# Second layer's experts: the bias of the down product by one f32r matmul of ones against its high and low parts

## The reference, cut to what matters

```python
def _L1_ffn_ref(x, Wr, W1, b1, W2, b2):
    B, T, D, F_FF, E, K = (8, 512, 256, 1024, 8, 2)
    pooled = x.mean(axis=1)
    logits = pooled @ Wr
    top_scores, top_idx = jax.lax.top_k(logits, K)
    weights = jax.nn.softmax(top_scores, axis=-1)
    W1s, b1s = (W1[top_idx], b1[top_idx])
    W2s, b2s = (W2[top_idx], b2[top_idx])
    h = jnp.einsum('btd,bkdf->bktf', x, W1s) + b1s[:, :, None, :]
    h = jax.nn.gelu(h, approximate=False)
    y = jnp.einsum('bktf,bkfd->bktd', h, W2s) + b2s[:, :, None, :]
    return jnp.einsum('bk,bktd->btd', weights, y)
```

## Time and profile before

| | before |
|---|---|
| runs (us) | 3388.6, 3382.0, 3391.19; median 3388.6 |
| the profiled execution: span (us) | 3419.0 |
| TensorE busy over the span | 3115.7 us, 91% |
| mean granted TensorE clock | 0.957 of full speed |
| this stage (first bias matmul to last) | 1389.14 to 1583.18 us |

### The profile page before, as it was taken

The page is one execution under the profiler, slowest core; times in us unless marked ns, Lnnn a source line. Parts: engine busy times, 40 slices in busy tenths (PEclk is TensorE's granted clock), DMA queues, the critical chain, the costliest instruction groups (busy, mean ns, idle before and its releaser), DMA issues. The chain is left out here.

```text
span 3419.0 us, 59989 instructions
## 1 busy us (share of the span) xinstructions
PE 3115.7 (91%) x23982; PEld 2628.8 (77%) x23993; DVE 1875.7 (55%) x3913; ACT 1705.1 (50%) x3695; POOL 1520.5 (44%) x1146
## 2 busy tenths in 40 slices
PE   6997999999698898998997989799997999889995
PEld 5776888888575565897665868678886888789995
DVE  4764222223566465776554754467775666565554
ACT  4763332332276554554654653356665666535553
POOL 0222344434212675674234651233334454539984
PEclk9998999999799999999998999899999999999998
DMA  1002000100000010442001010110001000036652
GB/s 65 3 11 79 19 19 19 38 1 1 23 3 23 1 50 1 149 168 75 3 3 43 8 50 1 39 50 1 1 1 38 6 6 1 26 115 217 223 181 74
DMA packets 49794, 156.96 MB, mean 46 GB/s; under 512 B 9322, under 2 KB 29438, under 8 KB 37104
## 3 DMA queue, kind: packets, MB, share of 16 engines
q1 hardware_dynamic: 45776, 142.90, 12.2%
q0 software_dynamic: 3744, 10.23, 1.0%
HBM read 142.06 MB, written 10.26 MB: 45 GB/s over the span
## 5 line engine op out<-in xcount | busy, mean ns | idle before, releaser
L1303 POOL TENSOR_TENSOR prob<-prob,inv 128x512 f32<-128x512 f32 x320 | 331.6, 1042 | 401.3 <-DVE inv L1355 391.8
L1193 ACT ACTIVATE prob<-banks,nmax 128x256 f32<-128x256 f32 x640 | 297.3, 474 | 155.1 <-DVE nmax L1349 155.0
L2682 POOL TENSOR_TENSOR hL<-product,hH 128x512 fp32r<-128x512 f32 x128 | 165.9, 1296 | 321.5 <-ACT hH L2629 321.5
L2288 DVE TENSOR_REDUCE nmax<-banks 128x4 f32<-128x1024 f32 (+1 forms) x192 | 217.5, 1133 | 153.7 <-PE banks L1870 85.9
L2727 DVE TENSOR_TENSOR product<-banks,silu 128x512 f32<-128x512 f32 x128 | 88.6, 692 | 388.6 <-PE banks L2553 333.4
L2621 ACT ACTIVATE silu<-banks 128x512 f32<-128x512 f32 x128 | 76.5, 598 | 367.6 <-PE banks L2553 367.6
L1349 DVE TENSOR_REDUCE nmax<-banks 128x2 f32<-128x512 f32 x320 | 215.4, 685 | 20.6 <-PE banks L1172 16.2
L2553 PE MATMUL banks<-xH,upH 128*128 128x512 f32 x512 | 202.1, 395 | 5.8 <-POOL upL L2669 5.8
L2553 PE MATMUL banks<-xL,upH 128*128 128x512 f32 x512 | 201.5, 394 | 0.0
L2553 PE MATMUL banks<-xH,upL 128*128 128x512 f32 x512 | 199.9, 390 | 0.0
L3364 ACT ACTIVATE banks<-banks 128x512 f32<-128x512 f32 x124 | 71.9, 584 | 213.9 <-PE banks L3308 186.8
(11 more groups left out here) (617 smaller groups left out, 11026.6 us busy)
## 6 DMA issues: line engine op xcount, KB each, us to landing
W<-in_L_ffn_experts SPq DMA_DIRECT2D x80, 1024.0 KB, 5.4
W<-in_L_ffn_experts SPq DMA_DIRECT2D x8, 1536.0 KB, 7.9
slots_y<-W SPq DMA_DIRECT2D x23, 256.0 KB, 6.1
W<-strips SPq DMA_DIRECT2D x4, 768.0 KB, 7.5
W<-in_L_ffn_experts SPq DMA_DIRECT2D x9, 256.0 KB, 4.9
X<-in_x SPq DMA_DIRECT2D x1, 2048.0 KB, 8.3
cs<-in_ctxT SPq DMA_DIRECT2D x16, 128.0 KB, 2.3
W<-in_L_ffn_experts SPq DMA_DIRECT2D x1, 2048.0 KB, 7.6
```

The costliest lines, as they stand in the source:

```text
L1193: ins = nc.scalar.activation(m_.prob[p % 2][:, e * 512 + j * S:e * 512 + (j + 1) * S], bank(key)[:, j * S:(j + 1) * S], ACT.Exp, bias=m_.n ...
L1303: nc.gpsimd.tensor_tensor(pr, pr, m_.inv[:, slot(p, e):slot(p, e) + 2].unsqueeze(2).to_broadcast([P, 2, S]), ALU.mult)\
L2288: nc.vector.tensor_reduce(m_.nmax[b % 2][:, 2 * parts * i_:2 * parts * (i_ + 1)].rearrange("p (e q) -> p e q", e=2), scores.rearrange("p e ...
L2682: nc.gpsimd.tensor_tensor(m_.hL[:, at], m_.product[s % 2][:, :], m_.hH[:, at].bitcast(F32), ALU.subtract).then_inc(g.h_low.sem, 1)
```

## The change

The row of ones becomes a full f32r tile `ones_rows` of 128x128. For each k a tile `b2[k]` of 128x256 f32r is cleared once, and for each unit its row 0 gets the high part of b2 (ScalarE) and its row 32 the low part: ScalarE first writes the high part there too, and GpSimd then subtracts it from b2. One f32r matmul of the ones against that tile, taken twice, adds up the rows. b2 is loaded into rows 0 and 32 of `bcast`, so there is one more small load for each unit. The two copies of ScalarE stand between hidden 0 and hidden 1. GpSimd's subtraction stands behind the low part of the down weights, with a wait for it and a wait for the copies ahead, and a wait for itself behind. TensorE waits for GpSimd's result in place of its wait for the small loads; its wait for the low part of the down weights stays.

```diff
--- before.py
+++ after.py
@@ -211,6 +211,7 @@
         self.split_high, self.values_low = sig("narrow_weights_high"), sig("value_weights_low")
         self.xt_high, self.packed = sig("inputs_high"), sig("identity_packed")
         self.res_biased = sig("residual_biased")
+        self.b2_cleared, self.b2_high, self.b2_low = sig("down_bias_cleared"), sig("down_bias_high"), sig("down_bias_low")
 
     def expert_memory(self, scope, name):
 
@@ -2818,6 +2819,8 @@
         self.upH, self.upL = [sb("upH0", 2048), sb("upH1", 2048)], [sb("upL0", 2048), sb("upL1", 2048)]
         self.downH, self.downL = [sb("downH0", 2048), sb("downH1", 2048)], [sb("downL0", 2048), sb("downL1", 2048)]
         self.hH, self.hL = sb("hH", 2048), sb("hL", 2048)
+        self.ones = sb("ones_rows", P)
+        self.b2 = [sb("b2_0", D), sb("b2_1", D)]
 
 
 def experts_by_batch(nc, g, name, n, scope):
@@ -2873,7 +2876,8 @@
                     filled(sp, ("y", j - 2))
                 sp.dma_start(g.cols[:, k * 8:k * 8 + 8], g.dram[f"{name}.b1"][ds(e, 1), :, :].rearrange("a p c -> (a p) c"))\
                     .then_inc(g.half_loaded[k].sem, 16)
-                sp.dma_start(g.bcast[0:1, k * D:(k + 1) * D], g.dram[f"{name}.b2"][ds(e, 1), :]).then_inc(g.half_loaded[k].sem, 16)
+                for row in (0, 32):
+                    sp.dma_start(g.bcast[row:row + 1, k * D:(k + 1) * D], g.dram[f"{name}.b2"][ds(e, 1), :]).then_inc(g.half_loaded[k].sem, 16)
                 if j == 1:
                     prefetch(nc, g, sp, n + 1)
 
@@ -2918,9 +2922,9 @@
                     transpose_x(b + 1)
                 split(pe, g.down_low, j)
                 to = claim(("y", j))
-                loaded(pe, g.half_loaded, j, 32)
-                nc.tensor.matmul(to[:, :].rearrange("p (t d) -> p t d", t=2), g.ones[:, :],
-                                 g.bcast[0:1, k * D:(k + 1) * D].unsqueeze(1).to_broadcast([1, 2, D]), start=True, stop=False)
+                split(pe, g.b2_low, j)
+                nc.tensor.matmul(to[:, :].rearrange("p (t d) -> p t d", t=2), m_.ones[:, :],
+                                 m_.b2[k][:, :].unsqueeze(1).to_broadcast([P, 2, D]), start=True, stop=False)
                 for f in range(8):
                     if f % 2 == 0:
 
@@ -2968,9 +2972,13 @@
             down_high(0)
             act.wait_ge(g.chosen_ready.sem, g.chosen_ready.base + 1)
             nc.scalar.activation(ex, ex, ACT.Exp).then_inc(g.act_step.sem, 1)
+            act.wait_ge(g.b2_cleared.sem, g.b2_cleared.base + 1)
             for j in range(NU):
-                loaded(act, g.half_loaded, j, 32)
+                loaded(act, g.half_loaded, j, 48)
                 hidden(j, 0)
+                for row in (0, 32):
+                    ins = nc.scalar.activation(m_.b2[j % 2][row:row + 1, :], g.bcast[row:row + 1, (j % 2) * D:(j % 2 + 1) * D], ACT.Copy)
+                ins.then_inc(g.b2_high.sem, 1)
                 hidden(j, 1)
                 if j + 1 < NU:
                     up_high(j + 1)
@@ -2987,6 +2995,9 @@
                 pool.wait_ge(g.var_ready.sem, g.var_ready.base + b + 1)
                 nc.gpsimd.tensor_tensor(g.rstd[:, 2 * b:2 * b + 2], g.vare[:, 2 * b:2 * b + 2], g.mhalf[:, 0:2], ALU.pow).then_inc(g.rstd_ready.sem, 1)
 
+            nc.gpsimd.memset(m_.ones[:, :].bitcast(F32), 1.0)
+            nc.gpsimd.memset(m_.b2[0][:, :].bitcast(F32), 0.0)
+            nc.gpsimd.memset(m_.b2[1][:, :].bitcast(F32), 0.0).then_inc(g.b2_cleared.sem, 1)
             for j in range(NU):
                 if j:
                     split(pool, g.up_high, j + PIECES - 1)
@@ -2996,6 +3007,11 @@
                 nc.gpsimd.tensor_tensor(m_.downL[j % 2][:, :], raw[j % 2][:, 2048:4096], m_.downH[j % 2][:, :].bitcast(F32), ALU.subtract)\
                     .then_inc(g.down_low.sem, 1)
                 b, k = divmod(j, 2)
+                split(pool, g.down_low, j)
+                split(pool, g.b2_high, j)
+                nc.gpsimd.tensor_tensor(m_.b2[k][32:33, :], g.bcast[32:33, k * D:(k + 1) * D], m_.b2[k][32:33, :].bitcast(F32), ALU.subtract)\
+                    .then_inc(g.b2_low.sem, 1)
+                split(pool, g.b2_low, j)
                 if k == 0 and b:
                     power(b - 1)
             power(B - 1)
@@ -3074,7 +3090,10 @@
     for k in range(2):
         g.up_loaded[k].base += 16 * B
         g.down_loaded[k].base += 16 * B
-        g.half_loaded[k].base += 32 * B
+        g.half_loaded[k].base += 48 * B
+    g.b2_cleared.base += 1
+    for sig in (g.b2_high, g.b2_low):
+        sig.base += NU
     g.var_ready.base += B
     g.rstd_ready.base += B
```

## The result

The changed kernel took 3368.13 us (median of 5 runs, 3364.47 to 3372.84), beside 3385.41 us (5 runs) of the kernel before: ratio 0.9944, 95% interval 0.993 to 0.9957. Two later comparisons, each on one chip, gave 0.9946 (0.9933 to 0.9958) and 0.9950 (0.9934 to 0.9965). By these ratios it is faster by 17 to 19 us (the medians lie 17.3, 20.2 and 17.8 us apart); forecast were 15.3 us, a time of 3373.3 us, and a range of 3366 to 3384.

A forecast was written before the change was run, and what follows sets the result against it. TensorE was taken to bound the experts' stage; a cheaper bias saves 7.2 us in seven units and 8.1 in eight, none in unit 0: 3388.6 - 15.3 = 3373.3 us, range 3366 to 3384.

The forecast's parts named there:

- What bounds it: Experts' stage: TensorE, busy for all 194.04 us between the first and last bias matmul, sets the time.
- The new matmul: TensorE's bias in each unit: one f32r matmul at 0.23 us replaces 1.26 or 1.24 us, saving 1.03 or 1.01.
- Rival 2: TensorE's bias: new matmul overlaps with nothing, 0.4 us per unit, 6.4 us less gain, 3379.7; chance 0.13 together with Rival 1.
- The copies: ScalarE between hidden 0 and hidden 1: two one-row copies, 0.72 us per unit, bounds 0 and 0.81, mostly hidden.
- The subtraction: GpSimd, one row of 256 per unit: 0.63 us, hidden with 1.9 us of slack before TensorE's bias in unit 3.
- VectorE's slack in unit 3: VectorE's low parts ahead of TensorE's down product: 0.4 us left for piece 0, 0.6 for piece 1, nothing late.
- Rival 1: Units with k = 1: VectorE or ScalarE becomes late, at worst 6 us lost, 3380; chance 0.13 together with Rival 2.
- Unit 0: First unit, where VectorE's first low part is late: no gain, taken as 0; a blocked small operation would lose 0.3 us.
- Sum: Whole stage: 7 x 1.03 plus 8 x 1.01 us, unit 0 nothing, 15.3 us saved.
- the 5 us allowed for the spread: Lower end of the time range: 5 us for run spread, beside the full saving and a lower matmul price, giving 3366.

The follow-up runs named there:

- e1: The changed kernel with TensorE's bias put back to the plain fp32 matmul of one row of ones; ratio to the kernel before 0.9995.
- e5: The changed kernel with its f32r bias matmul taking row 0 alone, low part left out of the result; ratio to the kernel before 0.997.
- e11: The changed kernel with its bias matmul reading the same 128-row tiles as plain fp32 instead of f32r; ratio to the kernel before 0.9977.
- e2: The changed kernel without its bias matmul, loads, copies, subtraction and waits kept; ratio to the kernel before 0.9947.
- e3: The changed kernel with each of ScalarE's two copies of b2 made twice, the second into an unread tile; ratio to the kernel before 0.9957.
- e6: The changed kernel with the high part of b2 alone: no second ScalarE copy, no GpSimd subtraction; ratio to the kernel before 0.9947.

## Why the prediction was right

- What bounds it: TensorE, without a gap in units 1 to 14, before and after. e1 shows it from the other side. Unit 0, and after the change the last unit too, follow VectorE.
- The new matmul: 0.23 us was taken from the twelve f32r matmuls, 0.23 was measured; 1.26 and 1.24 us for the old one, from the earlier trace rows, were right too. The words on why the old one cost more than its passes (loads that don't overlap) were right, but the cause was not named. e5 and e11 show it: the one row. Rival 2 had this mechanism at 0.4 us; a change to f32r with one row would have met it at 0.38. The size agrees by luck: the rival counted 0.2 us on each side, while 1.24 - 1.05 is 0.19 for both sides together. In e5 0.09 us stand ahead of the bias (0.21 in place of 0.12), 0.19 in its own pitch (0.42 in place of 0.23) and 0.10 behind the first down matmul. With 128 rows it doesn't come.
- The copies: 0.72 us forecast, 0.83 measured, above the upper bound of 0.81 by 0.02. The subtraction: 0.63 forecast, 0.74 measured. Both terms are hidden as said in units 1 to 14, with 1.6 us left for the subtraction in unit 3 where 1.9 was said.
- VectorE's slack in unit 3: 0.4 and 0.6 us forecast, 0.34 and 0.46 measured. Rival 1 did not happen there (in the last unit it did, for 0.2 us), but it begins 0.3 us away, as e2 and e3 show.
- Unit 0: forecast 0, measured a loss of 0.4 us. The step that was mis-sized is the choice against the rule. I had worked out 0.3 us by the rule of the Trainium skill, SBUF — State Buffer, section "Who interferes with whom", and left it out of the sum. The rule is the one that held: the operation with two SBUF inputs waited for GpSimd's subtraction (0.54 us in place of 0.17), the reciprocal ahead of it and the copies behind it kept their 0.16 to 0.20 us, and without the subtraction unit 0 is 15.61 us again (e6).
- The last unit: not in the forecast, 11.97 us in place of 11.75, since VectorE is late at its start. The sum also took unit 14 for one with transposes; it has none. The two belong together: unit 14 is 0.42 us shorter than the others with k = 0, and that is more than the 0.34 us that VectorE has left.
- Sum: forecast 15.3 us, in the traces 14.6 us; unit 0 and the last unit are 0.6 of the difference. The comparisons' 17 to 19 us lie above both, with part of the difference open. The time came out 5.2 us under the forecast of 3373.3: 3.2 of them are the kernel before, 3385.41 us over five runs where 3388.6 was carried over, and 2.0 are gain. That the time lies in the range is helped by the 5 us allowed for the spread.

A delay of VectorE that was not foreseen: its small operation on the variance now meets GpSimd's subtraction for the down weights.

```profile
1402.66 1.42 DVE L308 TENSOR_SCALAR vare<-meanvar 128x2 f32<-128x2 f32 x1
```

It took 0.17 us before. It ends at 1404.08, GpSimd's subtraction at 1404.06. It moves VectorE by 1.25 us at the head of each unit with k = 0, and is hidden there.

## What to carry to other kernels

A bias by a plain fp32 matmul of one row in a stream of full f32r matmuls costs twice here: by its type and by its row count, since the weight loads on both sides then stand alone. Filled with rows of zeros and kept in the type of the neighbours, it costs no more than an f32r matmul of as many columns; the preparation was free in units 1 to 14 because three other engines had 0.3 to 4 us of waiting in each, and cost 0.6 us in the first and the last. Before the bound engine is made shorter still, work out what the next engine has left at its tightest unit: here 0.34 us, and taking away 0.23 more in each unit returned only about a quarter of it over the stage.

## What the runs showed of the hardware

- The weight load of an f32r matmul with 128 rows like its neighbours starts with the matmul ahead (pitch 0.12 us for 256 columns, 0.23 for 512; trace of the changed kernel); that of one with 1 row beside 128 starts 0.21 us behind it (e5). The Trainium skill, TensorE: Matmul & The Clock Gate, section "Part 3: Packing small matmuls", states that loads overlap running matmuls only where their row groups differ, and in another place of the section that a load to the background weight buffer is pulled ahead too. The runs show loads of the same 128 rows overlapping, so the first statement does not hold by itself, and the measurement decides. Which buffer a load goes to, no run here shows.
- In e1 the granted clock fell inside unit 0, for 3.4 us, with TensorE busy throughout, after 0.46 us in which it had waited for VectorE. Windows of that trace, columns as in the result:

```profile
1382.64:1384.84 2.20, 1.74 (x7) 0.91 (x8) 2.10 (x5) 2.20 (x7) 1.74 (x1) 0.99 1.02 428
1384.84:1388.20 3.36, 3.36 (x18) 3.36 (x18) 3.29 (x6) 1.86 (x2) 3.36 (x2) 0.50 0.48 195
1388.20:1391.50 3.30, 3.30 (x29) 3.30 (x29) 0.51 (x1) 0.00 (x0) 3.30 (x1) 1.00 0.00 0
```

The middle one runs at the lower level of 1.2 GHz (0.50), its neighbours at 2.4 GHz. The pitch is 0.21 in place of 0.12 us there, and unit 0 took 17.23 us, 1.2 more than in the traces of the changed kernel, where the first low part comes as late. None of the other 13 traces shows the fall, though TensorE waits 0.9 to 1.2 us for VectorE at the same place in the three of the changed kernel. What calls it forth wasn't tried.
